# VectorE's slot reordered, and turned norms taken by ScalarE, in a four-layer attention and expert kernel

## The chip, the cores and the metric

One Trainium2 chip, one core. The metric is device time in microseconds of one execution. Each core has five engines with their own instruction streams: TensorE (PE), VectorE (DVE), ScalarE (ACT), GpSimd (POOL) and SyncE (SP, which here only issues DMAs). They meet at semaphores.

## The reference

The input is x of 32 sequences x 128 positions x 128 features, a condition vector per sequence and a context of 77 tokens per sequence. Four layers follow each other:

```python
# L0: self attention with rope and a mask, cross attention with the context, perceptron
x_norm = _ln(x, norm1_w) * (1 + sc_msa) + sh_msa
x = x + g_msa * self_out
xc = _ln(x, normc_w) * (1 + sc_x) + sh_x
x = x + g_x * cross
xm = _ln(x, norm2_w) * (1 + sc_mlp) + sh_mlp
x = x + g_mlp * (gelu(xm @ mlp_W1 + mlp_b1) @ mlp_W2 + mlp_b2)
# L1: evidence from the context, three routed experts, a gate
# L2: cross attention; queries and keys both from modulated norms
# L3: self attention, cross attention (of x without a norm), perceptron
```

Attention has 16 heads of 8 features, softmax over the keys. All is float32. Every modulated norm ends in a scale and a shift per feature and sequence.

## The kernel before

Four sequences make a quad; attention runs over 40 quads (5 attention layers x 8): l0 (128 keys, masked by the 128x128 mask, rope), l0c (77 keys, masked by a context mask), then, after the expert stage, l2 (77 keys), l3s (128 keys) and l3c (77 keys). The two phases are quads 0 to 15 and 16 to 39. Every engine has its own function `attention(phase, first, last)` that walks over slots t, one per sequence; `qi, cl = divmod(t, 4)` are the quad and the place in it (cl 0 to 3). Each engine's order within a slot is written out by hand, and semaphore waits tie the engines.

TensorE's slot t (lines 720 to 767): row scores of sequence t+5, half 1 (`rows`, L573: queries on partitions, only for the maxima); the exact scores of t transposed (`exact`, L604) and minus the maxima (`shift`, L616); row scores of t+6, half 0; `weigh` of t-1 (L631: probabilities times values). Then come `turn_max` at cl 3 (L581), and `quad_work`: at cl 0 the projection of the keys of quad qi+2 (L522, with rope also L525), at cl 1 the transpose of a norm (`turn_normed`, L490) or of x (L497), at cl 2 the values of qi+1 (L530) and the output projection of qi-2 (L537), at cl 3 the queries of qi+3 (L511, L514) and the transpose of a "family" norm (of the l2 context or of the two perceptrons). In the masked layer l0 the order is `quad_work` first and `weigh` and `turn_max` last. The two halves of row scores share two PSUM banks: `rows` waits until VectorE has taken the maximum of the half before it.

VectorE's slot t (lines 1227 to 1289): the maximum of t+5, half 1 (`row_max`, L1104); of t-2 the 32x32 block transpose of `weigh`'s result (`turn_blocks`, L1120); the transpose back of t-3 (`turn_back`, L1139); the reciprocal of the sums (`invert`, L1125); the maximum of t+6, half 0; at cl 3 `spread_max` (L1111, `nblk`); the product with the reciprocal (`normalise`, L1131, `attn`). Then `rotate` (rope, L1078 and L1082), `take_x` (L1068), `residual` at cl 2 (L1147, L1150), `take_q` at cl 3 (L1092, L1097), `scale_normed` (L1060) and `take_stats` (L978 and L983: four instructions each). In masked slots the first maximum stands behind `invert`, and `spread_max` behind the scaling.

A norm's way: `take_stats` on VectorE, Ln and Exp on ScalarE (`root`, L1454 and L1457), subtraction and product on GpSimd (`normalise_x`, L1679 and L1682), four transposes on TensorE into one PSUM bank (`turn_normed`), the scaling on VectorE from PSUM into `hat` (`scale_normed`), and the shift on GpSimd in the next slot from `hat` into the target (`shift_normed`, L1693). There are 56 of them: 24 in phase 0 and 32 in phase 1, 16 of those in phase 1 and 8 of those in phase 0 of the family kind. The PSUM bank is free again when `ln_scaled` has counted.

ScalarE's slot t: the exponentials of t (two instructions, L1508), taking keys (L1480, L1482) and values (L1498), `root`, `round_q` (L1471), taking queries (L1490). GpSimd's slot: `spread_q(t+1)` (L1655), adding the rotated half (L1672), `spread_k(t+7)` (L1665), `shift_normed`, `normalise_x`, adding bias rows or gated results (L1698, L1704).

The expert stage (`routed`, 10 iterations) lies between the phases; in its last iterations the first slots of phase 1 are interleaved by hand, on each engine at its own places. GpSimd cannot read PSUM here; all PSUM readers are VectorE and ScalarE.

Of the kernel before, what the change touches and what calls it, by code (L numbers as in the profile page):

```python
# [164 lines left out]
def build(nc, a, out_x):  # L165
    with ExitStack() as ctx:
# [62 lines left out]
        hat = sb("hat", [128, QUAD * S])  # L229
# [33 lines left out]
        ln_centred, ln_xhat, ln_turned, ln_scaled, ln_done = sem("ln_centred"), sem("ln_xhat"), sem("ln_turned"), sem("ln_scaled"), sem("ln_done")  # L263
# [183 lines left out]
        def tensor_program(e):  # L447
# [210 lines left out]
            def attention(phase, first=-16, last=None):  # L658
# [5 lines left out]
                def scores_read(t):  # L664

                    qi, cl = divmod(t, QUAD)
                    if cl == 0 and qi + 2 in quads and layer_of(qi + 2).rope:
                        w.wait_ge(rope_half, 4 * (qi + 2) + 4)
                    if t in norm_at and norm_at[t].family:
                        w.wait_ge(ln_scaled, norm_at[t].index + 1)  # L670
                    if cl == 2 and qi - 2 in quads and qi >= hi:
                        w.wait_ge(wo_read, qi - 1)
                    if cl == 2 and qi + 1 in quads:
                        w.wait_ge(v_done, qi + 2)
                    if cl == 3 and qi + 3 in quads and layer_of(qi + 3).rope:
                        w.wait_ge(rope_half, 4 * (qi + 3) + 2)

                def quads_read(t):

                    qi, cl = divmod(t, QUAD)  # L680
                    if cl == 0 and qi + 2 in quads:
                        if layer_of(qi + 2).rope:
                            w.wait_ge(rope_half, 4 * (qi + 2) + 3)
                        else:
                            w.wait_ge(k_done, qi + 2 - NB + 1)
                    if cl == 1 and qi + 3 in quads and layer_of(qi + 3).name == "l3c":
                        w.wait_ge(raw_done, (qi + 3) % NB + 1)
                    if t in norm_at and not norm_at[t].family:
                        w.wait_ge(ln_scaled, norm_at[t].index + 1)
# [169 lines left out]
            def routed():  # L859
# [8 lines left out]
                for i in range(NB + 2):  # L868
# [48 lines left out]
                    if last:  # L917
                        hidden_layer(c, 6)
                        if c == NB - 1:
                            w.wait_ge(ln_scaled, A_NORMS + 3)  # L920
                        gate_layer(c)
# [48 lines left out]
        def vector_program(e):  # L970
# [83 lines left out]

            def scale_normed(it):
                scale, _, ready, value = affine(it)
                w.wait_ge(ready, value)
                w.wait_ge(ln_turned, it.index + 1)
                w.wait_ge(ln_done, it.index)
                e.tensor_tensor(by_seq(hat[:, 0:it.cols]), by_seq(turned_bank(it)[:, 0:it.cols]),  # L1060
                                scale.unsqueeze(2).to_broadcast([128, QUAD, it.n]), ALU.mult).then_inc(ln_scaled, 1)
# [160 lines left out]
            def attention(phase, first=-16, last=None):  # L1222
# [3 lines left out]
                jobs, quads, norm_at = range(4 * lo, 4 * hi), range(lo, hi), NORM_AT[phase]  # L1226
                for t in range(4 * lo + first, end):
                    qi, cl = divmod(t, QUAD)
                    masked = t in jobs and layer_of(qi).mask == "qk"
                    if t + 5 in jobs and not masked:  # L1230
                        row_max(t + 5, 1)
                    if t - 2 in jobs:
                        turn_blocks(t - 2)
                    if t - 3 in jobs:
                        turn_back(t - 3)
                    if t - 2 in jobs:
                        invert(t - 2)
                    if t + 5 in jobs and masked:
                        row_max(t + 5, 1)
                    if t + 6 in jobs:  # L1240
                        row_max(t + 6, 0)
                    if cl == 3 and qi + 1 in quads and not masked:
                        spread_max(qi + 1)
                    if t - 2 in jobs:
                        normalise(t - 2)
                    if cl == 0 and qi + 2 in quads and layer_of(qi + 2).rope:
                        rotate(qi + 2, 1)
                    if cl == 1 and qi + 3 in quads and layer_of(qi + 3).name == "l3c":
                        take_x(qi + 3)
                    if cl == 2 and qi - 2 in quads:  # L1250
                        residual(qi - 2)
                    if cl == 3 and qi + 3 in quads:
                        if layer_of(qi + 3).rope:
                            rotate(qi + 3, 0)
                        elif not q_by_act(qi + 3):
                            take_q(qi + 3)
                    if t in norm_at:
                        scale_normed(norm_at[t])
                    if cl == 3 and qi + 1 in quads and masked:
                        spread_max(qi + 1)  # L1260
                    for it in STATS_AT.get((phase == 1, t), ()):
                        take_stats(it)
# [182 lines left out]
        def scalar_program(e):  # L1445
# [39 lines left out]

            def take_q(q):
# [25 lines left out]
            def attention(phase, first=-16, last=None):  # L1512
# [4 lines left out]
                for t in range(4 * lo + first, end):  # L1517
# [14 lines left out]
                    if cl == 2 and qi + 1 in quads:  # L1532
                        take_v(qi + 1)
                    for it in roots:
                        if not it.family:
                            root(it)
                    if cl == 1 and qi + 2 in quads:
                        round_q(qi + 2)
# [50 lines left out]
            for i in range(NB + 2):  # L1589
# [18 lines left out]
                if i + 1 < NB:  # L1608
                    routed_root(i + 1)
                if last:  # L1610
                    hidden_silu(c, 2)
                if now:
                    take_weights(i)
                if last:
# [3 lines left out]
                for k in (4, 5, 6):  # L1618
                    if last:
                        hidden_silu(c, k)  # L1620
                if last:
                    gate_sigmoid(c)
                if i == NB:
                    attention(1, -14, -7)
# [6 lines left out]
        def pool_program(e):  # L1631
# [53 lines left out]
            def shift_normed(it):  # L1685
                _, shift, ready, value = affine(it)
                w.wait_ge(ready, value)
                w.wait_ge(ln_scaled, it.index + 1)
                if it.kind in ("l2k", "l2", "l0", "l0c", "l3s"):
                    w.wait_ge(proj_v, it.q - 2)  # L1690
                    w.wait_ge(proj_q, it.q - 2)
                    w.wait_ge(proj_k, it.q - 2)
                e.tensor_tensor(by_seq(norm_target(it)), by_seq(hat[:, 0:it.cols]),  # L1693
                                shift.unsqueeze(2).to_broadcast([128, QUAD, it.n]), ALU.add).then_inc(ln_done, 1)

# [10 lines left out]
            def attention(phase, first=-16, last=None):  # L1706
# [4 lines left out]
                for t in range(4 * lo + first, end):  # L1711
# [9 lines left out]
                    if t - 1 in norm_at:  # L1721
                        shift_normed(norm_at[t - 1])
# [231 lines left out]
```

## Time and profile before

| | |
|---|---|
| median of 3 runs | 1201.91 us (1200.75 to 1204.64) |
| profiled execution | 1201.14 us, its span 1199.0 us |
| granted TensorE clock, mean | 0.954 |
| TensorE busy | 1068.0 us (89%) |
| VectorE busy | 821.1 us (68%) |
| ScalarE busy | 571.5 us (48%) |
| GpSimd busy | 598.0 us (50%) |
| chain that ended last | TensorE 66%, VectorE 20%, issue 7%, ScalarE 3%, GpSimd 3% |

Phase 0 takes about the first 400 us, the expert stage until about 675, phase 1 the rest. Busy shares are over the whole span. Matmul ends are modelled, and a busy TensorE is not TensorE at its peak; idle time of an engine costs only where others wait for it.

### The profile page before, as it was taken

The numbers are of one execution on the slowest core, as the hardware profiler recorded it, in microseconds if no ns is written. First come the engines' busy times: TensorE is split into PE (matmuls) and PEld (weight loads), VectorE is DVE, ScalarE is ACT, GpSimd is POOL, SyncE is SP. The second block draws the span as 40 slices with busy tenths as digits, with TensorE's granted clock in tenths as the row PEclk, the third lists the DMA queues.
The fourth block names the chain that finished last, engine by engine and source line by source line (L and its number), as shares of the span: only waits on it lengthen the run. The fifth ranks groups of instructions, "written<-read, shape, count | busy, mean of one in ns | idle before, by whom it ended". The sixth has DMA issues, their size and how long they took to land.

```text
span 1199.0 us, 28596 instructions
## 1 busy us (share of the span) xinstructions
PE 1068.0 (89%) x11711; PEld 674.1 (56%) x11711; DVE 821.1 (68%) x2035; ACT 571.5 (48%) x801; POOL 598.0 (50%) x602
## 2 busy tenths in 40 slices
PE   7899999999888997989999688899888999999898
PEld 4445545555554774656666445555555556655476
DVE  6677777778774433756677668788887887787521
ACT  1133334465556434443444236465555556665563
POOL 5565665566754331111114468576565645566421
PEclk8899999999999997998999769899999999998999
DMA  4300000000001102000000000000000000000001
GB/s 171 125 2 2 19 11 11 19 11 19 16 14 29 36 27 83 12 6 6 6 6 12 11 12 2 1 2 2 2 1 1 2 2 2 2 2 2 1 27 44
DMA packets 9280, 22.88 MB, mean 19 GB/s; under 512 B 1392, under 2 KB 1648, under 8 KB 8768
## 3 DMA queue, kind: packets, MB, share of 16 engines
q1 hardware_dynamic: 9152, 21.07, 5.3%
q8 instruction: 93, 1.52, 0.6%
q14 instruction: 35, 0.29, 0.1%
HBM read 18.90 MB, written 2.15 MB: 18 GB/s over the span
## 4 chain that ended last, share of the span: by engine, by line
PE 66%; DVE 20%; issue 7%; ACT 3%; POOL 3%; DMA 0%; DVEq 0%; SPq 0%; POOLq 0%; ACTq 0%
PE weighed L631 10%; DVE negmax L1104 9%; PE row_scores L573 6%; PE scores L777 5%; PE scores L604 5%; PE weighed L654 5%; PE scores L530 4%; PE quads L511 3%; PE quads L537 3%; PE quads L522 3%; PE row_scores L777 3%; DVE bn L978 2%; PE scores L616 2%; PE row_scores L788 2%; PE scores L644 2%
## 5 line engine op out<-in xcount | busy, mean ns | idle before, releaser
L1104 DVE TENSOR_REDUCE negmax<-row_scores 128x8 f32<-128x616 f32 (+1 forms) x312 | 298.6, 957 | 83.7 <-PE row_scores L573 52.4
L1508 ACT ACTIVATE p<-scores 128x1024 f32<-128x1024 f32 (+1 forms) x256 | 247.6, 1018 | 218.7 <-PE scores L616 218.7
L1665 POOL TENSOR_TENSOR kblk_r<-work,pack_const 128x308 fp32r<-128x308 f32 (+1 forms) x160 | 134.2, 839 | 240.7 <-PE row_scores L573 216.4
L604 PE MATMUL scores<-qblk,work 32*77 32x512 f32 (+1 forms) x1280 | 205.8, 626 | 13.9 <-ACT p L1508 6.8
L573 PE MATMUL row_scores<-kblk_r,qr 32*128 32x308 f32 (+1 forms) x624 | 141.9, 444 | 54.3 <-DVE negmax L1104 51.6
L631 PE MATMUL weighed<-p,v 77*32 77x128 f32 (+1 forms) x5120 | 176.1, 279 | 2.7 <-DVE nat L1120 2.5
L1655 POOL TENSOR_TENSOR qblk<-work,pack_const 128x512 f32<-128x512 f32 x160 | 168.7, 1054 | 14.6 <-PE scores L604 13.6
L573 PEld LDWEIGHTS row_scores<-kblk_r,qr 32*128 32x128 f32 x624 | 63.8, 189 | 176.0 <-issue 101.9
L631 PEld LDWEIGHTS weighed<-p,v 77*32 77x32 f32 (+1 forms) x5120 | 132.1, 111 | 45.7 <-DVE nat L1120 22.0
L616 PE MATMUL scores<-nblk,select 32*77 32x512 f32 (+1 forms) x640 | 154.9, 808 | 0.0
L1508 ACT ACTIVATE p<-scores,neg_kb 77x1024 f32<-77x1024 f32 x64 | 67.6, 1105 | 52.3 <-PE scores L616 52.3
L604 PEld LDWEIGHTS scores<-qblk,work 32*77 32x77 f32 (+1 forms) x1280 | 63.0, 161 | 22.5 <-ACT p L1508 9.6
L1120 DVE STREAM_TRANSPOSE nat<-weighed 128x256 f32<-128x256 f32 x160 | 70.2, 439 | 6.1 <-PE weighed L631 6.1
L1131 DVE TENSOR_TENSOR attn<-nat,rden 128x128 f32<-128x128 f32 x160 | 72.6, 454 | 0.5
L1679 POOL TENSOR_TENSOR xh<-x,mv 128x512 f32<-128x512 f32 x48 | 50.1, 1043 | 45.4 <-ACT rst L1457 45.4
L1748 POOL TENSOR_TENSOR xh<-x,r_mv 128x512 f32<-128x512 f32 x8 | 8.3, 1044 | 109.4 <-ACT r_rst L1465 109.4
L654 PEld LDWEIGHTS weighed<-layers_w,work 128*128 128x128 f32 x512 | 59.0, 192 | 5.3 <-issue 3.3
L654 PE MATMUL weighed<-layers_w,work 128*128 128x128 f32 x512 | 60.0, 275 | 1.6 <-DVE x L1168 0.8
L616 PEld LDWEIGHTS scores<-nblk,select 32*77 32x77 f32 (+1 forms) x640 | 47.3, 163 | 23.7 <-issue 13.5
L1682 POOL TENSOR_TENSOR xh<-xh,rst 128x512 f32<-128x512 f32 (+1 forms) x56 | 58.3, 1041 | 4.4
L511 PE MATMUL quads<-work,layers_w 128*128 128x512 f32 x80 | 49.2, 700 | 0.0
L1498 ACT COPY v<-scores 77x512 f32<-77x512 f32 (+1 forms) x40 | 23.4, 584 | 49.6 <-PE scores L530 49.6
(287 smaller groups left out, 1841.9 us busy)
## 6 DMA issues: line engine op xcount, KB each, us to landing
shared<-gates_hbm SPq DMA_DIRECT2D x24, 256.0 KB, 3.2
shared<-in_ctx_tok SPq DMA_DIRECT2D x16, 154.0 KB
pack_w_l<-in_w_l SPq DMA_DIRECT2D x1, 2058.5 KB, 10.0
x<-in_x_tok SPq DMA_DIRECT2D x8, 256.0 KB, 6.2
out_x<-x SPq DMA_DIRECT2D x8, 256.0 KB, 2.0
layers_w<-in_w_l SPq DMA_DIRECT2D x1, 1289.0 KB, 9.1
ctxT<-in_ctxT SPq DMA_DIRECT2D x1, 1232.0 KB, 8.8
layers_w<-in_w_l SPq DMA_DIRECT2D x1, 640.0 KB, 6.4
```

The source lines that it names most:

```text
L511: e.matmul(quad_bank[:, :], W[layer.wq], xn[q % 3], start=True, stop=True).then_inc(proj_q, 1)
L573: mm = e.matmul(row_banks(n, h)[:, i, 0:cols], qr[q % 3][at, s * S:(s + 1) * S], kblk_r[n % 2][at, 0:cols], start=layer.mask is None or ma ...
L604: mm = e.matmul(scores[0:nk, g, :], k_of[q % 3][at, s * nk:(s + 1) * nk], qblk[n % 2][at, :], start=layer.mask != "qk", stop=False, skip_g ...
L616: mm = e.matmul(scores[0:nk, g, :], select[at, s, 0:nk], nblk[q % 2][at, :], start=False, stop=True, skip_group_check=True, tile_position= ...
L631: mm = e.matmul(av_bank[TILE * j:TILE * j + TILE, i2 * S:(i2 + 1) * S], v[0:nk, at:at + TILE], p[n % 2][0:nk, g * NJ + j, :], start=i1 == ...
L654: mm = e.matmul(mlp_out_bank[:, s * D:(s + 1) * D], mlp_h[c % 2][k][:, s * S:(s + 1) * S], W[weight][:, k * D:(k + 1) * D], start=(k == 0) ...
L777: mm = e.matmul(bank, weight, src, start=(part == 0), stop=(part == 1))
L1104: e.tensor_reduce(negmax[q % 2][:, 2 * h:2 * h + 2, 0, s * NJ:(s + 1) * NJ], row_banks(n, h)[:, :, 0:NJ * nk].rearrange("p g (j k) -> p g ...
L1131: e.tensor_tensor(attn[n % 2][:, :].rearrange("p (k d) -> p k d", d=HD), nat[n % 2][:, :, :].rearrange("p i (k c) -> p (i k) c", c=16)[:, ...
L1508: e.activation(p[n % 2][0:nk, 8 * h:8 * h + 8, :], scores[0:nk, 2 * h:2 * h + 2, :].rearrange("p g (j q) -> p (g j) q", j=NJ), ACT.Exp, bi ...
L1655: e.tensor_tensor(qblk[n % 2][:, :].rearrange("p (j s) -> p j s", j=NJ), q_of[q % 3][:, s * S:(s + 1) * S].unsqueeze(1).to_broadcast([128, ...
L1665: e.tensor_tensor(kblk_r[n % 2][:, 0:NJ * nk].rearrange("p (j k) -> p j k", j=NJ), k_of[q % 3][:, s * nk:(s + 1) * nk].unsqueeze(1).to_bro ...
```

## The change

On VectorE the slot gets one order for masked and unmasked slots: both maxima first; then `rotate` for keys and for queries, `spread_max`; then the evacuation, of t-1 instead of t-2 (and the transpose back of t-2 instead of t-3), with reciprocal and `normalise` directly behind it; then `take_stats`; then `take_x`, `residual` and `take_q`. `scale_normed` is gone from VectorE and `shift_normed` from GpSimd. In their place ScalarE has `take_normed`: four activations per norm (one per sequence, 128 or 77 columns, scale and bias per partition) straight from PSUM into the target, behind the exponentials, `take_k`, `take_v` and `round_q` of the slot. TensorE waits for `ln_done` where it waited for `ln_scaled`. `round_q` moves ahead of the roots that are not of the family. In the expert stage ScalarE's slots -14 to -7 of phase 1 are spread between the activations of the last but one iteration.

```diff
@@ vector_program, attention @@
-                    masked = t in jobs and layer_of(qi).mask == "qk"
-                    if t + 5 in jobs and not masked:
-                        row_max(t + 5, 1)
-                    if t - 2 in jobs:
-                        turn_blocks(t - 2)
-                    if t - 3 in jobs:
-                        turn_back(t - 3)
-                    if t - 2 in jobs:
-                        invert(t - 2)
-                    if t + 5 in jobs and masked:
+                    if t + 5 in jobs:
                         row_max(t + 5, 1)
                     if t + 6 in jobs:
                         row_max(t + 6, 0)
-                    if cl == 3 and qi + 1 in quads and not masked:
-                        spread_max(qi + 1)
-                    if t - 2 in jobs:
-                        normalise(t - 2)
                     if cl == 0 and qi + 2 in quads and layer_of(qi + 2).rope:
                         rotate(qi + 2, 1)
+                    if cl == 3 and qi + 3 in quads and layer_of(qi + 3).rope:
+                        rotate(qi + 3, 0)
+                    if cl == 3 and qi + 1 in quads:
+                        spread_max(qi + 1)
+                    if t - 1 in jobs:
+                        turn_blocks(t - 1)
+                    if t - 2 in jobs:
+                        turn_back(t - 2)
+                    if t - 1 in jobs:
+                        invert(t - 1)
+                        normalise(t - 1)
+                    for it in STATS_AT.get((phase == 1, t), ()):
+                        take_stats(it)
                     if cl == 1 and qi + 3 in quads and layer_of(qi + 3).name == "l3c":
                         take_x(qi + 3)
                     if cl == 2 and qi - 2 in quads:
                         residual(qi - 2)
-                    if cl == 3 and qi + 3 in quads:
-                        if layer_of(qi + 3).rope:
-                            rotate(qi + 3, 0)
-                        elif not q_by_act(qi + 3):
-                            take_q(qi + 3)
-                    if t in norm_at:
-                        scale_normed(norm_at[t])
-                    if cl == 3 and qi + 1 in quads and masked:
-                        spread_max(qi + 1)
-                    for it in STATS_AT.get((phase == 1, t), ()):
-                        take_stats(it)
+                    if cl == 3 and qi + 3 in quads and not layer_of(qi + 3).rope and not q_by_act(qi + 3):
+                        take_q(qi + 3)
@@ scalar_program @@
+            def take_normed(it):
+                scale, shift, ready, value = affine(it)
+                w.wait_ge(ready, value)
+                w.wait_ge(ln_turned, it.index + 1)
+                if not it.kind in ("l0m", "l3f"):
+                    w.wait_ge(proj_v, it.q - 2)
+                    w.wait_ge(proj_q, it.q - 2)
+                    w.wait_ge(proj_k, it.q - 2)
+                for s in range(QUAD):
+                    at = slice(s * it.n, (s + 1) * it.n)
+                    done = e.activation(norm_target(it)[:, at], turned_bank(it)[:, at], ACT.Identity, bias=shift[:, s:s + 1],
+                                        scale=scale[:, s:s + 1])
+                done.then_inc(ln_done, 1)
@@ scalar_program, attention @@
+                    if cl == 1 and qi + 2 in quads:
+                        round_q(qi + 2)
+                    if t in norm_at:
+                        take_normed(norm_at[t])
                     for it in roots:
                         if not it.family:
                             root(it)
-                    if cl == 1 and qi + 2 in quads:
-                        round_q(qi + 2)
@@ scalar_program, expert stage @@
+                if i == NB:
+                    attention(1, -14, -12)
                 if last:
                     hidden_silu(c, 2)
...
                 if i == NB:
-                    attention(1, -14, -7)
+                    attention(1, -8, -7)
@@ tensor_program, four places @@
-                        w.wait_ge(ln_scaled, norm_at[t].index + 1)
+                        w.wait_ge(ln_done, norm_at[t].index + 1)
@@ pool_program @@
-                    if t - 1 in norm_at:
-                        shift_normed(norm_at[t - 1])
```

## Rows read from the trace of the kernel before

**Rows 1.** Waits of TensorE, whole span: waiting, releaser: total us, times, longest.
```profile
PE row_scores L573 <- DVE negmax L1104: 51.6, 75, 2.8
...
PE scores L604 <- DVE hat L1060: 6.4, 7, 1.1
```

**Rows 2.** Timeline in l3s, cl 2 to cl 0: start, us, engine, line, tiles, idle before.
```profile
880.94 0.50 PE L573 MATMUL row_scores<-kblk_r,qr 32*128 32x512 f32 x2 [0.66 <-DVE negmax L1104]
...
884.36 0.50 PE L573 MATMUL row_scores<-kblk_r,qr 32*128 32x512 f32 x2
...
884.47 0.69 DVE L1150 TENSOR_TENSOR x<-quads,x 128x512 f32<-128x512 f32 x1 [1.57 <-PE quads L537]
...
886.27 1.19 DVE L1104 TENSOR_REDUCE negmax<-row_scores 128x8 f32<-128x1024 f32 x1
...
887.61 0.50 PE L573 MATMUL row_scores<-kblk_r,qr 32*128 32x512 f32 x2 [1.65 <-DVE negmax L1104]
...
889.42 0.69 DVE L1111 TENSOR_TENSOR nblk<-weighed,pack_const 128x512 fp32r<-128x512 f32 x1
...
890.17 0.49 PE L573 MATMUL row_scores<-kblk_r,qr 32*128 32x512 f32 x2
...
890.71 1.23 DVE L1104 TENSOR_REDUCE negmax<-row_scores 128x8 f32<-128x1024 f32 x1 [0.40 <-PE row_scores L573]
...
890.75 1.04 POOL L1665 TENSOR_TENSOR kblk_r<-work,pack_const 128x512 fp32r<-128x512 f32 x1 [3.77 <-PE row_scores L573]
...
891.85 0.44 DVE L1120 STREAM_TRANSPOSE nat<-weighed 128x256 f32<-128x256 f32 x1
...
892.08 0.50 PE L573 MATMUL row_scores<-kblk_r,qr 32*128 32x512 f32 x2 [0.32 <-DVE negmax L1104]
...
894.58 0.50 PE L573 MATMUL row_scores<-kblk_r,qr 32*128 32x512 f32 x2
```

**Rows 3.** Timeline at the end of phase 0, VectorE without row maxima.
```profile
367.81 0.45 DVE L1120 STREAM_TRANSPOSE nat<-weighed 128x256 f32<-128x256 f32 x1 [1.25 <-PE weighed L631]
...
368.62 0.29 DVE L1131 TENSOR_TENSOR attn<-nat,rden 128x128 f32<-128x128 f32 x1
...
368.83 0.86 DVE L978 BATCH_NORM_STATS2 bn<-x 128x6 f32<-128x128 f32 x4
```

**Rows 4.** Timeline late in l3c: a product beside a GpSimd operation.
```profile
1105.27 1.27 POOL L1698 TENSOR_TENSOR x<-x,rows_bc 128x512 f32<-128x512 f32 x1
...
1105.58 1.10 DVE L1131 TENSOR_TENSOR attn<-nat,rden 128x128 f32<-128x128 f32 x1
```

**Rows 5.** Timeline in the masked layer l0, from cl 2 to the next quad.
```profile
142.49 1.08 PE L631 MATMUL weighed<-p,v 128*32 128x128 f32 x32
...
144.05 0.50 PE L573 MATMUL row_scores<-kblk_r,qr 32*128 32x512 f32 x2
...
145.06 1.16 DVE L1104 TENSOR_REDUCE negmax<-row_scores 128x8 f32<-128x1024 f32 x1
...
146.37 0.50 PE L573 MATMUL row_scores<-kblk_r,qr 32*128 32x512 f32 x2 [0.73 <-DVE negmax L1104]
...
150.44 0.69 DVE L1111 TENSOR_TENSOR nblk<-weighed,pack_const 128x512 fp32r<-128x512 f32 x1 [0.51 <-PE weighed L581]
...
151.47 1.04 POOL L1665 TENSOR_TENSOR kblk_r<-work,pack_const 128x512 fp32r<-128x512 f32 x1 [0.18 <-PE row_scores L573]
```

**Rows 6.** Groups by shape, whole span: busy us, mean ns, idle before.
```profile
L1104 DVE TENSOR_REDUCE negmax<-row_scores 128x8 f32<-128x616 f32 x188 | 148.3, 789 | 36.2 <-PE row_scores L573 34.9 <-PE scores L573 1.1
...
L1490 ACT ACTIVATE work<-quads,layers_w 128x512 f32<-128x512 f32 x21 | 14.4, 688 | 34.8 <-PE quads L511 34.8
...
L1454 ACT ACTIVATE logv<-mv,eps_col 128x4 f32<-128x4 f32 x48 | 14.1, 294 | 30.2 <-DVE mv L983 30.1
```

**Rows 7.** Timeline, end of phase 1 and expert stage: two waits.
```profile
1133.06 1.08 PE L631 MATMUL weighed<-p,v 77*32 77x128 f32 x32 [1.23 <-DVE nat L1120]
...
659.98 0.46 PE L490 MATMUL scores<-pack_const,xh 77*128 77x77 f32 x4 [2.28 <-POOL xh L1682]
```

More of the change, by code:

```diff
@@ L228, in build @@
         xh = [sb(f"xh{f}", [128, QUAD, D]) for f in range(2)]
-        hat = sb("hat", [128, QUAD * S])
         gated = [sb(f"gated{i}", [128, QUAD * D]) for i in range(2)]
@@ L262, in build @@
         ln_bn, ln_stats, ln_log, ln_rstd = ([sem(f"{s}{f}") for f in range(2)] for s in ("ln_bn", "ln_stats", "ln_log", "ln_rstd"))
-        ln_centred, ln_xhat, ln_turned, ln_scaled, ln_done = sem("ln_centred"), sem("ln_xhat"), sem("ln_turned"), sem("ln_scaled"), sem("ln_done")
+        ln_centred, ln_xhat, ln_turned, ln_done = sem("ln_centred"), sem("ln_xhat"), sem("ln_turned"), sem("ln_done")
         raw_turned, raw_done = sem("raw_turned"), sem("raw_done")
@@ L688, in quads_read @@
                     if t in norm_at and not norm_at[t].family:
-                        w.wait_ge(ln_scaled, norm_at[t].index + 1)
+                        w.wait_ge(ln_done, norm_at[t].index + 1)
                     if cl == 2 and qi - 2 in quads and qi < hi:
@@ L919, in routed @@
                         if c == NB - 1:
-                            w.wait_ge(ln_scaled, A_NORMS + 3)
+                            w.wait_ge(ln_done, A_NORMS + 3)
                         gate_layer(c)
@@ L1053, in setup_gates @@
                 e.tensor_copy(live_bc[:, :], av_bank[:, 3 * D + B:3 * D + 2 * B]).then_inc(dve_setup, 1)
[L1055 to L1061, printed above, removed]
             def take_x(q):
@@ L1225, in attention @@
                 end = 4 * hi + TAIL if last is None else 4 * lo + last
-                jobs, quads, norm_at = range(4 * lo, 4 * hi), range(lo, hi), NORM_AT[phase]
+                jobs, quads = range(4 * lo, 4 * hi), range(lo, hi)
                 for t in range(4 * lo + first, end):
                     qi, cl = divmod(t, QUAD)
-                    masked = t in jobs and layer_of(qi).mask == "qk"
-                    if t + 5 in jobs and not masked:
-                        row_max(t + 5, 1)
-                    if t - 2 in jobs:
-                        turn_blocks(t - 2)
-                    if t - 3 in jobs:
-                        turn_back(t - 3)
-                    if t - 2 in jobs:
-                        invert(t - 2)
-                    if t + 5 in jobs and masked:
+                    if t + 5 in jobs:
                         row_max(t + 5, 1)
@@ L1613, in scalar_program @@
                     take_weights(i)
+                if i == NB:
+                    attention(1, -12, -10)
                 if last:
@@ L1617, in scalar_program @@
                     take_evidence(i)
-                for k in (4, 5, 6):
-                    if last:
-                        hidden_silu(c, k)
                 if last:
+                    hidden_silu(c, 4)
+                    hidden_silu(c, 5)
+                if i == NB:
+                    attention(1, -10, -8)
+                if last:
+                    hidden_silu(c, 6)
                     gate_sigmoid(c)
                 if i == NB:
-                    attention(1, -14, -7)
+                    attention(1, -8, -7)
                 if i + 1 < NB:
@@ L1683, in normalise_x @@
                                 ALU.mult).then_inc(ln_xhat, 1)
[L1685 to L1694, printed above, removed]
             def add_rows(c, row, done):
```

## The prediction

> **What bounds the kernel now.** I read the waits of TensorE first, then the groups by shape, then the timeline of single slots. TensorE is busy 89% of the span, and its largest wait by far is for a row maximum of VectorE: 51.6 us in 75 waits, then 6.4 us for the scaled norm [rows 1]. So the kernel is TensorE in its fixed order, plus what VectorE is late. A slot has two couplings: the row scores of half 1 open it, the row scores of half 0 of the next sequence stand behind `exact` and `shift`, and the second may not start before the maximum of the first is taken.
>
> I measure in a 128-key slot of the third-phase self attention [rows 2]. Row scores begin at P = 890.17; the maximum can begin at P + 0.54 (890.71); the second row scores begin 1.37 after it (892.08). With VectorE on time the second pair starts at Q = P + 1.91. Each microsecond that VectorE comes after P + 0.54 is a microsecond of TensorE: at P = 884.36 the maximum starts at 886.27, 1.37 late, and the second pair at 887.61 instead of 886.27, with 1.65 idle [rows 2]. So the question is: when is VectorE free, relative to P + 0.54 of the next slot?
>
> **The change part by part.** *Order.* Before, the evacuation (transpose, transpose back, reciprocal) of sequence t-2 stands in the gap between the two maxima, where VectorE would wait for TensorE anyway: a maximum advances it 1.14 (890.71 to 891.85), and the next one can start only at Q + 0.54, that is 1.91 after the last began, a gap of 0.8. After, that gap is empty and the evacuation of t-1 follows the second maximum. Its length is read where nothing disturbs it: transpose at 367.81, `attn` at 368.62 (0.81 later, 0.29 long), the next instruction at 368.83: 1.02 in all [rows 3]. VectorE is then free at Q + 0.54 + 1.14 + 1.02 = Q + 2.70. Four slots of a quad, with P' the next slot's start:
> - cl 0: P' = Q + 2.50 (894.58), limit Q + 3.04: on time, before and after.
> - cl 1: P' = Q + 2.02 by the same view, limit Q + 2.56: 0.14 late; before, with the 0.60 of the scaling, 0.34.
> - cl 2: P' = Q + 3.42 (880.94 to 884.36), limit Q + 3.96. Before: residual from 0.11 after the end slot begins (884.47), then statistics (0.90 + 0.30 by cadence), maximum 1.37 late. After: statistics go ahead, into the wait for the output projection, then the residual 0.60: free at Q + 2.70 + 1.20 + 0.60 = Q + 4.50, 0.54 late. This is the gain of the change: 0.83.
> - cl 3: before on time. After, `nblk` (at Q + 1.81, 889.42) comes first, 0.60, and the 1.02 behind it: free at Q + 3.43 against 3.10, 0.33 late.
> By this alone a quad gains 0.7 us.
>
> *Contention.* But `attn` now begins at Q + 1.81 + 0.60 + 0.81 = Q + 3.22, which is P' + 0.66 (P' = 890.17), and GpSimd's key spread starts at P' + 0.58 (890.75) and runs 1.04. A normal `attn` takes 0.29; the one at 1105.58 that met a GpSimd operation (1105.27 for 1.27) took 1.10 and ended 0.14 after it [rows 4]. So `attn` ends at P' + 1.76, and VectorE is free at P' + 1.68, 1.14 late in place of 0.33. The margin is 0.08 us, so both values stay as bounds. The Trainium skill (SBUF — State Buffer, Summary: rules for kernel authors) states it outright: a VectorE operation with two SBUF inputs and a GpSimd operation that reads SBUF block each other fully, the second to issue waiting. The trace agrees (1.10 against 0.29) [rows 4]; if instead `attn` issued first, the rule would give the 0.33.
>
> *The same by layer*, lateness per quad before and after:
> - l0 (masked, 8 quads). Here `weigh` is TensorE's last work of a slot, so the evacuation waits for it, and all that is queued behind comes later still. cl 2: `weigh` ends at 142.49 + 1.08 = 143.57; evacuation from 143.61 to 144.63, statistics to 145.83, residual to 146.43, limit 144.05 + 0.54 = 144.59: 1.84 late, where before the maximum started at 145.06, 0.47 late (idle 0.73) [rows 5]. cl 3: `nblk` at 150.44 as before, then the transpose at 151.04 and `attn` at 151.85, inside the key spread of 151.47: free at 152.58, 1.16 late against 0.31. Sum 3.1 against 0.86: 2.25 x 6 = 13.5. The first two quads have no residual: 2.0 x 2 = 4.0. Three quads take Q at the very end of cl 3: 0.6 x 3 = 1.8. In all +19.3.
> - l0c (77 keys; a maximum advances VectorE 0.70 by its 789 ns [rows 6]). The limit rule is the same with zero slack. Four quads win at cl 2 (1.41 to 0.5) and lose at cl 3 (`nblk`, evacuation, taking Q); where statistics fall on cl 1 they now add to the whole evacuation (0.2 to 1.2). About -1.4.
> - l2: the four late quads 1.71 to 1.45, two 2.9 to 1.8, the first two (no residual) +0.7 each: -1.8.
> - l3s: 1.71 to 1.80 in four quads, +0.9 in one, and three quads that have `take_x` at cl 1 and no statistics, 0.37 to 2.04: +6.3.
> - l3c: `take_x` now stands behind the evacuation (0.26 to 0.68) and cl 3 costs 0.82: three quads +1.25, two +0.43, two with statistics alone +1.0: +6.6.
>
> *The four activations.* No 128-column activation from PSUM is in the trace. From below it is 0.29 (the 4-column one), from above 0.69 (512 columns) [rows 6]; linear between them, 0.39, and 0.28 from start to start as far as the two overlap: 4 cost 1.2, bounds 0.8 and 2.8. The Trainium skill (ScalarE: Activation LUTs, Rules for kernel authors) gives 0.3 us plus 0.83 ns per element, 0.41 each, so 1.6 for four, an estimate; the sum would be some 0.4 us per place that waits higher. The scalings are in the working above (0.60 of VectorE's queue, as `nblk`); GpSimd's shifts had nothing waiting. ScalarE has room between two exponentials except in 77-key slots, where rounding Q plus four activations end some 0.5 after the next exponential could start and `project_v` waits 0.2: 8 places, 1.6. Family norms hold a scores bank that `exact` waits for: before 1.1 from the turn to the scaled copy, now 1.35; about 6 places, 1.5. Sum +3.1, bounds 0 and +20.
>
> *Ends and the routed stage.* At the end of each phase a `weigh` waits 1.23 for a transpose queued behind a scaling [rows 7]; the transpose now comes a slot sooner: -2.4, and -1.0 for a GpSimd shift before the last perceptron. In the routed stage the turn of a norm waits 2.28 for GpSimd [rows 7], of which one shift (1.0) goes, and two scalings leave VectorE's last chain: -2.0. The start waits 0.5 longer for the first norm.
>
> Sum: 19.3 - 1.4 - 1.8 + 6.3 + 6.6 + 3.1 - 3.4 - 2.0 + 0.5 = +27. The profiled execution took 1201.14 (span 1199.0 and 2.1 around it); the median is 1201.91. Forecast 1228, own range 1217 to 1240.
>
> **The rivals.**
> 1. *No collision on the port.* The margin of 0.08 falls the other way, or GpSimd, relieved of 56 shifts, keeps clear. Then cl 3 costs 0.33 (0.4 with 77 keys): 6.6 less in l3s, 4.2 in l0, 4.0 in the other three: +12, 1214. For it: the small margin in l3s. Against: 0.38 of overlap in l0.
> 2. *Maxima first serves TensorE* (faster). The place is cl 2: if the statistics really vanish into the wait for the output projection and the evacuation fits behind the second maximum everywhere, waits above the 0.32 that each 128-key slot has by structure go. The waits for maxima are 51.6, of which some 60 x 0.32 = 19 stay; taking half of the other 33, and 5 of the 6.4, it is -21: 1180. It decides once VectorE's free time stays under Q + 3.0; my count has it over in cl 2 and cl 3.
> 3. *ScalarE becomes a bound*: activations of 0.69 each, 2.8 per norm, would meet the exponentials at 56 places with 0.2 to 1.5: +12 on the forecast, 1240. Against: 0.29 for a small one.
> 4. *No change*: gains and losses cancel, 1202. For it: l0c and l2 do cancel.
>
> **How the numbers follow.** Forecast 0.46, rival 1 0.25, rival 3 0.09, rival 2 0.13, rival 4 0.07. The range leaves out the faster case and the top of rival 3: 1203 to 1242. Within 0.3% (3.6 us) is what a measurement can't tell from no change. Faster 0.13, same 0.06, slower 0.81.
>
> **What would show it.** In the masked layer the maximum of half 1 after cl 2 starts 1.8 after its row scores end, not 0.5, and TensorE's wait there grows from 0.73 to about 2.1; the quad is 2.2 longer. In l3s the quads with statistics keep their length, with the wait at cl 3 down from 1.65 to 0.85 and that at cl 0 up from 0.32 to 1.4, behind an `attn` of about 1.1. TensorE's waits for maxima rise from 51.6 to above 75 in all. VectorE's busy time falls by some 38, GpSimd's by 58, and ScalarE's rises by 224 x 0.39 = 87. I am wrong if the masked quad does not grow, since 19 of the 27 lie there.

## The result, and the profile after

The changed kernel takes 1318.45 us (1314.34 to 1323.98, 4 runs) against 1203.15 of the kernel before (4 runs): ratio 1.0963, 95% interval 1.0917 to 1.101. It is 115 us slower, where 27 were forecast. The profiled execution has a span of 1317.6 us; the granted clock falls from 0.954 to 0.912.

The page of the changed kernel: busy time by engine, and the chain that ended last.

```profile
PE 1122.1 (85%) x11711; PEld 702.3 (53%) x11711; DVE 815.7 (62%) x1979; ACT 648.6 (49%) x1025; POOL 544.6 (41%) x546
...
PE 61%; DVE 24%; issue 7%; ACT 5%; POOL 3%; DMA 0%; DVEq 0%; ACTq 0%; POOLq 0%
```

TensorE runs the same 11711 matmuls, and is busy 54.1 us longer with them. That is the first half of the loss. The second is in the waits (engine, line, tile, what it waited for, total us, times, longest). First TensorE's, then VectorE's:

```profile
PE row_scores L572 <- DVE negmax L1095: 99.3, 84, 3.2
PE row_scores L567 <- DVE negmax L1095: 26.6, 18, 2.5
...
PE scores L603 <- ACT normT L1479: 6.5, 6, 1.8
```

```profile
DVE attnT L1130 <- PE quads L536: 53.3, 30, 3.2
```

The first two rows, together 125.9, answer to the 51.6 of [rows 1] and to this row of the kernel before, for masked row scores, whose first matmul is another line:

```profile
PE row_scores L568 <- DVE negmax L1104: 9.4, 10, 1.3
```

Before it was 61.0 in all. The waits for maxima rise by 64.9, and 64.9 + 54.1 = 119.0 is, within 0.4, the 118.6 by which the span grew. VectorE's row is new: before, its transpose back never waited for the output projection; there it was the residual that did.

Stretches by layer, each from one `nblk` to another, for l0, l0c, l2, l3s, l3c. The l0 line ends with the `nblk` of l0's last quad and the l0c line with that of l0c's last, so that the last masked quad is counted in the l0c line. The l2 and l3s lines run from a layer's first `nblk` to that of the next layer, the l3c line to its last quad. Columns: stretch, length, busy us of the engines, granted clock, DMA share, GB/s. Before:

```profile
52.34:219.62 167.28, 153.55 (x2391) 84.91 (x2390) 126.42 (x261) 65.07 (x85) 98.78 (x94) 0.99 0.05 13
219.62:363.81 144.19, 129.91 (x1915) 80.38 (x1909) 111.15 (x292) 80.56 (x104) 91.97 (x98) 0.98 0.05 16
...
697.34:848.15 150.81, 134.98 (x1707) 80.20 (x1706) 119.81 (x308) 84.39 (x119) 103.10 (x109) 0.93 0.01 3
848.15:1001.24 153.09, 136.10 (x1737) 85.36 (x1736) 123.11 (x248) 83.01 (x104) 88.55 (x87) 0.98 0.01 2
1001.24:1116.95 115.71, 110.03 (x1515) 68.51 (x1514) 87.06 (x219) 69.43 (x89) 71.66 (x75) 0.97 0.01 2
```

After:

```profile
57.58:249.91 192.33, 162.18 (x2379) 88.29 (x2379) 127.01 (x252) 74.94 (x113) 92.20 (x87) 0.93 0.03 9
249.91:420.82 170.91, 143.89 (x1915) 87.85 (x1910) 111.42 (x284) 92.83 (x140) 82.41 (x88) 0.88 0.05 13
...
752.53:923.91 171.38, 145.80 (x1707) 87.10 (x1706) 115.99 (x296) 101.86 (x173) 91.73 (x96) 0.86 0.01 2
923.91:1098.53 174.62, 144.49 (x1737) 89.55 (x1737) 128.50 (x243) 89.99 (x124) 83.59 (x82) 0.92 0.01 2
1098.53:1232.92 134.39, 115.19 (x1515) 71.99 (x1514) 90.91 (x216) 73.51 (x101) 68.37 (x72) 0.94 0.01 2
```

Every line is 19 to 27 us longer, not that of the masked layer alone, and in each TensorE's busy time grows with the length. With all eight quads (52.34 to 238.74 before, 57.58 to 273.54 after) the masked layer goes from 186.4 to 216.0, and l0c without the masked quad from 125.1 to 147.3.

The slot at fault, in l3s (timeline of the changed kernel, cl 2 to cl 0, the counterpart of [rows 2]):

```profile
985.00 1.06 PE L536 MATMUL quads<-layers_w,attnT 128*128 128x128 f32 x8
...
985.99 0.50 PE L572 MATMUL row_scores<-kblk_r,qr 32*128 32x512 f32 x2
...
986.16 0.31 DVE L1130 STREAM_TRANSPOSE attnT<-attn 128x128 f32<-128x128 f32 x1 [1.48 <-PE quads L536]
...
986.57 1.04 POOL L1671 TENSOR_TENSOR kblk_r<-work,pack_const 128x512 fp32r<-128x512 f32 x1 [3.39 <-PE row_scores L572]
986.65 1.11 DVE L1122 TENSOR_TENSOR attn<-nat,rden 128x128 f32<-128x128 f32 x1
...
987.68 0.86 DVE L977 BATCH_NORM_STATS2 bn<-x 128x6 f32<-128x128 f32 x4
...
988.87 0.66 DVE L1141 TENSOR_TENSOR x<-quads,x 128x512 f32<-128x512 f32 x1
...
989.45 1.21 DVE L1095 TENSOR_REDUCE negmax<-row_scores 128x8 f32<-128x1024 f32 x1
...
990.81 0.50 PE L572 MATMUL row_scores<-kblk_r,qr 32*128 32x512 f32 x2 [3.23 <-DVE negmax L1095]
...
992.80 1.92 PE L510 MATMUL quads<-work,layers_w 128*128 128x512 f32 x2
```

`attnT` has two buffers. At cl 2 the order of before turned back the last sequence of quad qi-1, into the buffer whose projection (that of quad qi-3) had long been done. The new order is one sequence ahead: at cl 2 it turns back the first sequence of quad qi, into the buffer that the output projection of quad qi-2 still reads, and TensorE issues that projection at the end of this very slot. So VectorE stands idle from 984.68 to 986.16, and only then do the transpose back, reciprocal, `attn` (1.11, beside the key spread), statistics and residual run, all in a row. The maximum, which could begin at 985.99 + 0.54 = 986.53, begins 2.92 late.

Behind this wait the two matmuls of the query projection take 1.92. In the kernel before they took 1.02 behind a wait of 1.65:

```profile
889.22 1.02 PE L511 MATMUL quads<-work,layers_w 128*128 128x512 f32 x2
```

The stretches of two microseconds there, in the changed kernel (last column but two is the granted clock):

```profile
987.00:989.00 2.00, 0.57 (x8) 0.00 (x0) 1.97 (x10) 1.57 (x2) 1.65 (x2) 1.00 0.02 4
989.00:991.00 2.00, 0.19 (x2) 0.21 (x2) 1.66 (x2) 0.76 (x3) 0.00 (x0) 1.00 0.00 0
991.00:993.00 2.00, 2.00 (x36) 1.38 (x35) 1.22 (x1) 0.00 (x0) 0.00 (x0) 0.72 0.04 8
993.00:995.00 2.00, 2.00 (x7) 0.50 (x9) 1.67 (x5) 0.25 (x1) 0.00 (x0) 0.50 0.00 0
995.00:997.00 2.00, 1.68 (x16) 0.93 (x12) 1.23 (x1) 1.05 (x2) 1.48 (x2) 0.92 0.00 0
```

TensorE is idle from 987.58 to 990.81. The row scores at 990.81 still take 0.50. From about 991.9 to about 995.2, although TensorE is fully busy, the clock stands at its lower level (0.50 of 2.4 GHz, that is 1.2 GHz). The wait costs its 3.23 us, and the matmuls that follow it take longer on top.

### The profile page after: what moved, and what is told of

It reads as the page before. It is cut to its first block, busy times and chain, and to the rows that moved or that the text cites. A ratio compares the mean times of both kernels' runs of the same rounds, so it can differ in the third digit from the quotient of the medians.

```text
span 1317.6 us, 28587 instructions
## 1 busy us (share of the span) xinstructions
PE 1122.1 (85%) x11711; PEld 702.3 (53%) x11711; DVE 815.7 (62%) x1979; ACT 648.6 (49%) x1025; POOL 544.6 (41%) x546
## 3 DMA queue, kind: packets, MB, share of 16 engines
q8 instruction: 93, 1.52, 0.5%
## 4 chain that ended last, share of the span: by engine, by line
PE 61%; DVE 24%; issue 7%; ACT 5%; POOL 3%; DMA 0%; DVEq 0%; ACTq 0%; POOLq 0%
PE weighed L630 12%; DVE negmax L1095 8%; PE row_scores L572 5%; PE scores L776 5%; PE scores L603 4%; PE weighed L653 4%; PE scores L529 4%; PE quads L510 3%; PE quads L536 3%; DVE bn L977 3%; PE quads L521 2%; PE row_scores L776 2%; DVE attn L1122 2%; DVE nat L1111 2%; ACT p L1505 2%
## 5 line engine op out<-in xcount | busy, mean ns | idle before, releaser
L572 PE MATMUL row_scores<-kblk_r,qr 32*128 32x308 f32 (+1 forms) x624 | 149.7, 469 | 102.5 <-DVE negmax L1095 99.3
L603 PE MATMUL scores<-qblk,work 32*77 32x512 f32 (+1 forms) x1280 | 220.4, 663 | 13.8 <-ACT p L1505 6.7
L630 PE MATMUL weighed<-p,v 77*32 77x128 f32 (+1 forms) x5120 | 191.5, 295 | 3.5 <-ACT normT L1479 3.5
L572 PEld LDWEIGHTS row_scores<-kblk_r,qr 32*128 32x128 f32 x624 | 67.6, 202 | 229.3 <-issue 171.0
L630 PEld LDWEIGHTS weighed<-p,v 77*32 77x32 f32 (+1 forms) x5120 | 143.0, 117 | 55.3 <-issue 51.2
L615 PE MATMUL scores<-nblk,select 32*77 32x512 f32 (+1 forms) x640 | 161.4, 833 | 0.0
L1505 ACT ACTIVATE p<-scores,neg_kb 77x1024 f32<-77x1024 f32 x64 | 67.5, 1105 | 54.6 <-PE scores L615 54.6
L603 PEld LDWEIGHTS scores<-qblk,work 32*77 32x77 f32 (+1 forms) x1280 | 69.5, 173 | 22.6 <-ACT p L1505 9.6
L1130 DVE STREAM_TRANSPOSE attnT<-attn 128x128 f32<-128x128 f32 x160 | 44.5, 278 | 53.4 <-PE quads L536 53.3
L615 PEld LDWEIGHTS scores<-nblk,select 32*77 32x77 f32 (+1 forms) x640 | 50.9, 171 | 25.8 <-issue 15.1
L510 PE MATMUL quads<-work,layers_w 128*128 128x512 f32 x80 | 61.5, 862 | 0.0
L1688 POOL TENSOR_TENSOR xh<-xh,rst 128x512 f32<-128x512 f32 (+1 forms) x56 | 58.2, 1039 | 4.4
```

The costliest lines, as they stand in the source:

```text
L510: e.matmul(quad_bank[:, :], W[layer.wq], xn[q % 3], start=True, stop=True).then_inc(proj_q, 1)
L572: mm = e.matmul(row_banks(n, h)[:, i, 0:cols], qr[q % 3][at, s * S:(s + 1) * S], kblk_r[n % 2][at, 0:cols], start=layer.mask is None or ma ...
L603: mm = e.matmul(scores[0:nk, g, :], k_of[q % 3][at, s * nk:(s + 1) * nk], qblk[n % 2][at, :], start=layer.mask != "qk", stop=False, skip_g ...
L615: mm = e.matmul(scores[0:nk, g, :], select[at, s, 0:nk], nblk[q % 2][at, :], start=False, stop=True, skip_group_check=True, tile_position= ...
L630: mm = e.matmul(av_bank[TILE * j:TILE * j + TILE, i2 * S:(i2 + 1) * S], v[0:nk, at:at + TILE], p[n % 2][0:nk, g * NJ + j, :], start=i1 == ...
L1505: e.activation(p[n % 2][0:nk, 8 * h:8 * h + 8, :], scores[0:nk, 2 * h:2 * h + 2, :].rearrange("p g (j q) -> p (g j) q", j=NJ), ACT.Exp, bi ...
```

## The experiments

Each ran beside the kernel before on its own chip (1200.16 us for the first four, 1200.84 for the next four, 1201.04 for the last three).

**1. Three buffers for attnT** (the changed kernel otherwise).

```diff
-        attnT = [sb(f"attnT{i}", [128, QUAD * S]) for i in range(2)]
+        attnT = [sb(f"attnT{i}", [128, QUAD * S]) for i in range(3)]
-                w.wait_ge(wo_done, q - 1)          # and attnT[q % 2] -> attnT[q % 3]
+                w.wait_ge(wo_done, q - 2)
```

> The changed kernel with a third attnT buffer, so that the transpose back of a quad's first sequence no longer waits in cl 2 for the output projection two quads back. Theory A (this wait, overlooked in the prediction, moves statistics and residual of the four unmasked layers behind the output projection): the 53.3 us that VectorE waits for L536 go to under 5, TensorE's wait at cl 3 of l3s goes from 3.2 to about 0.9, the four unmasked layers lose some 2 us per quad x 30 = 60 and the half-clock stretches behind these waits another 10 to 25, the masked layer keeps its 192 us: 1225 to 1255. Theory B (the loss is the order as such, evacuation behind both maxima, and the port): the wait only changes its name, over 1295.

Measured 1254.8 us (ratio 1.0457, 1.0422 to 1.0493): 64 us of the loss gone with one tile (61 if each is compared with the kernel before on its own chip, 54.6 above it in place of 115.3). VectorE's transpose back no longer waits for the output projection; the residual does, for 15.6 us in all. The l3s slots of this run (timeline), cl 2 to cl 0:

```profile
963.21 0.27 DVE L1130 STREAM_TRANSPOSE attnT<-attn 128x128 f32<-128x128 f32 x1
...
965.06 0.66 DVE L1141 TENSOR_TENSOR x<-quads,x 128x512 f32<-128x512 f32 x1
...
965.63 1.21 DVE L1095 TENSOR_REDUCE negmax<-row_scores 128x8 f32<-128x1024 f32 x1
...
966.99 0.50 PE L572 MATMUL row_scores<-kblk_r,qr 32*128 32x512 f32 x2 [0.81 <-DVE negmax L1095]
...
970.21 1.12 DVE L1122 TENSOR_TENSOR attn<-nat,rden 128x128 f32<-128x128 f32 x1
...
972.61 0.50 PE L572 MATMUL row_scores<-kblk_r,qr 32*128 32x512 f32 x2 [1.47 <-DVE negmax L1095]
```

This is the slot that the prediction described: 0.85 forecast for the first wait, 0.81 found; 1.4 behind an `attn` of 1.1 for the second, 1.47 and 1.12 found. The lengths of l0c, l2, l3s and l3c come down by 19.0, 20.3, 17.4 and 6.3; l0, which has no such wait, keeps its 192.3.

**2. The norms alone** (before's order on VectorE without the scaling, the activations on ScalarE, with the rest of what the change does on ScalarE, GpSimd and TensorE) and **3. the order alone** (the new order on VectorE, scaling and shift left with VectorE and GpSimd).

> VectorE's order as before the change, the norms by the four activations on ScalarE and nothing on GpSimd, as after it. If ScalarE's activations are harmless, as predicted: 1190 to 1205, 34 us less on VectorE's queue giving a few us back at cl 1. If they are a main cause of the loss: over 1240.

> VectorE's order as after the change, norms scaled on VectorE (at the end of the slot) and shifted on GpSimd as before. If the order is the whole loss: 1310 to 1345 (the scaling adds 0.6 behind the evacuation at cl 1). If order and activations share the loss: under 1290.

Measured 1193.05 (ratio 0.9942, 0.992 to 0.9964) and 1340.72 (1.1157, 1.111 to 1.1204). The order is the whole loss, and what moves to ScalarE is a small gain on either side: 7 us by itself, 22 within the new order (25 by the differences to the kernel before). VectorE's busy time falls by 38.4 with the norms alone, exactly the forecast 38; that the changed kernel shows only 5.4 less is therefore due to the order. Of the missing 33 us, 12 are a longer `attn` (475 ns mean against 401) and 3 other instructions. The other 18 are no work: neighbouring instructions overlap less. The durations of all of VectorE's instructions add to 858.4 for 782.7 of busy time in experiment 2 and to 873.0 for 815.7 in the changed kernel.

**4. More work for TensorE, none taken away**: in the changed kernel a helper issues `matmul(bank, ident, ones)` four times (eight matmul records in the trace, results overwritten) in each of 28 slots, ahead of `exact` at cl 3 of the unmasked layers, just before TensorE's wait for the maximum, so that the wait becomes shorter.

```diff
+                if s == 3 and layer.mask != "qk" and q + 2 < (2 * NB if q < 2 * NB else NQ):
+                    keep_busy(4, scores[:, 0, 0:128])
                 for g in range(NG):
```

> The changed kernel with four more 128x128 matmuls per quad on TensorE, ahead of exact at cl 3 of the unmasked layers, whose results are overwritten. They lie within the 3.2 us that TensorE waits there for a row maximum. If the idle stretch brings TensorE's half clock behind it (theory C, granted clock 0.88 in l0c and 0.86 in l2 against 0.98 and 0.92 before): the clock of the unmasked layers rises by 0.03 or more, the masked layer stays at 0.93, and the time falls by 8 to 30 us although work is added: 1290 to 1310. If the clock has another cause: unchanged clock, 1318 to 1325.

Measured 1300.75 (ratio 1.0855, 1.0792 to 1.0918): 18 us less with 224 matmuls more (15 less by the differences to the kernel before on either chip; the two 95% intervals of the ratio only just touch). Granted clock and length: l0c from 0.88 to 0.97 and 170.9 to 161.2, l2 from 0.86 to 0.97 and 171.4 to 159.4, l3s from 0.92 to 0.97 and 174.6 to 171.2, l3c from 0.94 to 0.96, less than the 0.03 expected, while l0, which got none, has 0.91 and 194.8. In l3s the wait behind the filler is still 1.9 in five quads, and the query projection behind it takes 1.92, 1.82, 1.79 and 1.26 in four of them, 1.02 in the fifth. TensorE's busy time is within 0.6 that of the changed kernel (1122.7), with the added work in it.

**5. Key spread kept behind attn** (on top of three buffers).

```diff
                 w.wait_ge(rows_done, 2 * n - 2)
+                w.wait_ge(attn_done, n - 8)
                 e.tensor_tensor(kblk_r[n % 2]...
```

> On top of the three attnT buffers (1254.8 us): GpSimd's key spread additionally waits until VectorE's attn of the same stretch is written, so that the two no longer read SBUF side by side. Theory A (collision on the port): with three buffers the slot of the third-phase self attention at cl 0 has the wait of 1.47 us behind an attn of 1.12 us beside a key spread; kept apart, attn takes 0.29 and the maximum can start up to 0.75 sooner, once per quad in the 128-key layers, some 32 quads x 0.4 to 0.75 = 13 to 24 us with what the clock gives back: 1231 to 1242, the waits for maxima (95 us) down to about 80. Theory B (the collision only shifts idle time): the spread itself comes late and TensorE waits for kblk_r in its place: 1250 or more, with waits for kblk_r above 10 us.

Measured 1233.32 (1.0274, 1.0236 to 1.0313), 21 us less than experiment 1. The same slots (timeline):

```profile
950.62 0.29 DVE L1122 TENSOR_TENSOR attn<-nat,rden 128x128 f32<-128x128 f32 x1
950.83 1.22 DVE L1095 TENSOR_REDUCE negmax<-row_scores 128x8 f32<-128x1024 f32 x1
951.06 1.04 POOL L1672 TENSOR_TENSOR kblk_r<-work,pack_const 128x512 fp32r<-128x512 f32 x1 [3.43 <-DVE attn L1122]
...
952.19 0.49 PE L572 MATMUL row_scores<-kblk_r,qr 32*128 32x512 f32 x2 [0.64 <-POOL kblk_r L1672]
```

`attn` is back to 0.29 and the wait of 1.47 is 0.64. Both theories hold in part: the waits for maxima fall from 95.1 to 63.0 (about 80 expected), but those for `kblk_r` rise from 1.9 to 21.4 in 43. What the Trainium skill says of this port (SBUF — State Buffer, Summary: rules for kernel authors), that the second to issue waits out the first, agrees with 1.12 (experiment 1, where the spread had started at 970.14 and `attn` at 970.21) against 0.29 for the same instruction.

**6. The masked slots' evacuation as before** (on top of three buffers: for t in l0, `turn_blocks(t - 2)`, `turn_back(t - 3)` and `invert(t - 2)` ahead of the maxima again, `normalise(t - 2)` behind them; at the first slot of l0c both orders meet).

> On top of the three attnT buffers (1254.8 us): in the 32 masked slots of the first layer alone the evacuation is that of sequence t-2 again and stands ahead of the maxima, as in the kernel before; the rest of the order stays new. Theory A (the order costs the masked layer 19 us, because weigh is TensorE's last work of a slot and the evacuation of t-1 behind it holds the next maximum): the first layer falls from 192.3 to 167 to 175 us, and the whole to 1230 to 1238. Theory B (the loss of the masked layer comes from nblk, the rotation halves or the norms, not from the evacuation): the layer stays above 185 and the whole above 1247.

Measured 1228.34 (1.0223, 1.0185 to 1.0261), 26 us less than experiment 1 and 2 below the expected range. All of it is in the masked layer, whose line is:

```profile
61.22:224.44 163.22, 149.79 (x2379) 83.59 (x2379) 121.20 (x251) 74.94 (x113) 91.84 (x87) 1.00 0.03 10
```

That is 29.0 less than in experiment 1; with all eight quads it is 33.3 less (215.8 to 182.5).

**7 and 8. The kernel before with the statistics ahead of the residual**, and the same with the norms on ScalarE.

```diff
+                    for it in STATS_AT.get((phase == 1, t), ()):
+                        take_stats(it)
                     if cl == 2 and qi - 2 in quads:
                         residual(qi - 2)
...
-                    for it in STATS_AT.get((phase == 1, t), ()):
-                        take_stats(it)
```

> The kernel before with one edit: the statistics of the norms stand ahead of the residual in the slot instead of last. Theory A (what the change rightly saw: at cl 2 VectorE waits for the output projection with nothing to do, then runs residual and statistics in a row, so that the maximum is 1.37 us late): the statistics, 1.20 us, fit into that wait, the maximum is at most 0.2 late, and some 25 quads gain 0.8 to 1.2 us: 20 to 30 us less, 1172 to 1182. Theory B (the residual then comes later and wo_read or the next norm's chain takes the place of the wait): no change, 1196 to 1206.

> The kernel before with the statistics ahead of the residual and the turned norms scaled and shifted by four activations on ScalarE, VectorE's order otherwise as before. Theory A: both gains add, that of the norms alone being 7 us (0.6 us less of VectorE's queue at each norm) and that of the statistics alone 20 to 30: 1163 to 1175. Theory B: with the statistics out of the way the scaling no longer stands in the critical slot, so that the norms give nothing more: the same as with the statistics alone, within 3 us.

Measured 1169.84 (0.9739, 0.9709 to 0.9769) and 1167.17 (0.9715, 0.9687 to 0.9743). One move of two lines gives 31 us, 2 more than the range expected. In experiment 8 (timeline, l3s, cl 2 to cl 3):

```profile
884.57 0.87 DVE L977 BATCH_NORM_STATS2 bn<-x 128x6 f32<-128x128 f32 x4
...
886.22 0.69 DVE L1141 TENSOR_TENSOR x<-quads,x 128x512 f32<-128x512 f32 x1 [0.37 <-PE quads L536]
...
886.83 1.22 DVE L1095 TENSOR_REDUCE negmax<-row_scores 128x8 f32<-128x1024 f32 x1
...
888.19 0.50 PE L572 MATMUL row_scores<-kblk_r,qr 32*128 32x512 f32 x2 [0.49 <-DVE negmax L1095]
```

The statistics lie inside the wait for the projection, and the 1.65 of [rows 2] is 0.49. This is the gain that the prediction credited to the change at cl 2; before's evacuation order lets it happen. The norms on ScalarE add 2.7 us, within the 3 of theory B and with overlapping intervals; the same kernel measured 1164.63 as experiment 10. Once the slot at cl 2 is free, moving the scaling gains at most a few us. These two are the fastest versions measured.

**9. All three repairs at once** (three buffers, key spread behind `attn`, masked slots as before).

> The changed kernel with all three repairs at once: three attnT buffers, the key spread held until attn is written, the masked slots with the old evacuation. Theory A (three separate causes, with the prices that the single runs gave: 64 us, 21 us, 26 us): they add, 1318 - 64 - 21 - 26 = 1207, between 1202 and 1214; what then stays over the 1193 of the old order with the norms on ScalarE is the evacuation at cl 3 and in 77-key slots. Theory B (they share the same waits, so that the repairs overlap): above 1216.

Measured 1210.63 (1.0073, 1.0051 to 1.0096): they add. The three causes are separate and account for 108 of the 115 us (106 by the differences to the kernel before). What stays over the 1193.05 of experiment 2, the old order with the norms on ScalarE, was not taken apart by a run. By the traces it lies in the start (+7.5) and in the 77-key layers (l0c +6.9, l2 +3.5, l3c +7.4), while l3s and the masked layer are 3.3 and 2.5 shorter.

**10 and 11. What a late maximum costs.** In experiment 11, on top of the kernel of experiment 8:

```diff
+                    if cl == 3 and t + 6 in jobs and not masked:
+                        for k in range(7):
+                            e.tensor_reduce(pad[:, 2 * k:2 * k + 2], cos_live[:, :, :], AX_X, ALU.max)
                     if t + 5 in jobs and not masked:
                         row_max(t + 5, 1)
```

Experiment 10 is the yardstick, the kernel of experiment 8 once more.

> The kernel with the statistics ahead of the residual and the norms on ScalarE, unchanged: the yardstick for the next run, in the same call. Theory A and B alike: 1163 to 1171.

> The kernel with the statistics first and the norms on ScalarE, and in the unmasked slots of cl 3 seven reductions of a 256-element table into a scratch tile ahead of the maximum of half 1: VectorE is late by some 2.3 us at this one slot of each of 32 quads (0.3 each by cadence, from 0.79 us for 616 elements), as in the changed kernel behind the transpose back. Nothing else changes. Theory A (a wait of 2 to 3 us costs more than its length, since TensorE's matmuls after it run at half clock): the waits give 32 x 2.3 = 74 us and TensorE's busy time grows by another 20 to 40, 1262 to 1282. Theory B (a wait costs its length): 1235 to 1245, TensorE's busy time within 5 us of 1056.5.

Measured 1164.63 and 1274.56 (1.0605, 1.0569 to 1.0641). Timeline of experiment 11:

```profile
958.71 2.37 DVE L1224 TENSOR_REDUCE pad<-cos_live 128x2 f32<-128x256 f32 x7
...
962.36 0.79 PE L573 MATMUL row_scores<-kblk_r,qr 32*128 32x512 f32 x2 [2.77 <-DVE negmax L1096]
...
965.21 1.91 PE L511 MATMUL quads<-work,layers_w 128*128 128x512 f32 x2
```

TensorE's waits for maxima, experiment 10 first, then experiment 11:

```profile
PE row_scores L572 <- DVE negmax L1095: 30.0, 69, 2.2
...
PE row_scores L573 <- DVE negmax L1096: 78.1, 70, 2.8
PE row_scores L568 <- DVE negmax L1096: 15.2, 8, 2.4
```

The 32 delays of 2.37 (two of them ahead of the masked layer) are 76 us of VectorE; the kernel is 110 us slower, and its profiled execution, the slowest of the four, 117. TensorE waits 62.5 us more for maxima (30.8, with 0.8 for masked row scores, to 93.3) and is busy 58.2 us longer with the same matmuls (1056.8 to 1115.0), more than the 20 to 40 of theory A. The mean granted clock goes from 0.966 to 0.918. So about half of what a wait of 2 to 3 us costs here is not the wait but the lower clock behind it.

## Why the prediction was wrong

The direction was right, the size was 27 against 115.

- **The step that failed: cl 2 of the unmasked layers.** "After: statistics go ahead, into the wait for the output projection, then the residual 0.60: free at Q + 2.70 + 1.20 + 0.60 = Q + 4.50, 0.54 late." In the trace the maximum there is 2.92 late. I had checked each moved instruction against the maxima and the port, but not the transpose back against its own waits. Moving it one sequence ahead moved it across a quad boundary of a two-buffered tile, so that at cl 2 the evacuation waits for the same projection as the residual. The statistics stand between the two and cannot fill the wait. Price with what follows from it: 64 us (experiment 1). With that wait away the slot is the one forecast, to 0.07 us.
- **A cost with no term: the clock.** The rule "Each microsecond that VectorE comes after P + 0.54 is a microsecond of TensorE" is too low. With three buffers the waits for maxima are 34.1 above before (61.0 to 95.1), near the 29.0 of my five layer terms, but TensorE's busy time is up another 23.1 and the kernel 54.6 longer. It could have been read from the kernel before: its l2 stands at 0.93, and in l3s the two matmuls of the query projection, 1.02 in most quads, take 1.76 at 868.65 and 1.52 at 910.10.
- **Masked layer, +19.3.** Right as to mechanism: the wait behind cl 2 is 2.14 (at 161.08; forecast 2.1), that of cl 0 1.46 (at 170.27) behind an `attn` of 0.81. Over its eight quads the waits for maxima rise by 20.5 (13.6 to 34.1), near the 19.3, and with the lower clock (0.99 to 0.93) the length by 29.6: 3.7 per quad where 2.2 were forecast. Experiment 6 takes back 33.3.
- **l3s +6.3, l3c +6.6.** With three buffers the waits rise by 5.3 and 6.7. Right as to waits.
- **l0c -1.4, l2 -1.8.** Even with three buffers l0c, without the masked quad, is +2.9 in waits (7.5 to 10.4) and l2 +0.6: small as forecast, but wrong in sign.
- **The port.** Right in the masked layer and in experiment 1. In the changed kernel itself it struck at cl 2, since the late transpose back pushed `attn` onto the key spread (986.57 and 986.65), and not at cl 0 (994.46, 0.29).
- **Four activations, +3.1.** 0.46 each, four in a row 1.5, near the 1.6 worked out from the Trainium skill (ScalarE: Activation LUTs, Rules for kernel authors) and above my 0.39 and 1.2. As a whole the norms are a gain of 7 (experiment 2): I had counted the relief of VectorE only inside the new order. ScalarE did not become a bound (rival 3). ScalarE's busy time rises by 77 (forecast 87), GpSimd's falls by 53 (58).
- **Start and ends.** The start, up to the first `nblk`, is 5.2 longer (0.5 forecast). In experiment 6, with the same order there as the changed kernel, it is 61.2 against 57.6, so that I leave its cause open. The last 82.0 became 84.7, where -3.4 for both ends was forecast; between the phases -1.8 (-2.0 forecast).

## What to carry to other kernels

When work is moved by one item within a software pipeline, list the semaphore that each moved instruction waits for, with its index at every position of the loop, and look for the index that crosses a buffer's boundary; one more buffer may be the whole repair. A wait already present is filled by moving independent work ahead of the waiting instruction, not by moving the waiting chain. And a wait of TensorE of 2 to 3 us, as here, is priced with the matmuls behind it, not by its length alone.

## What was not expected of the hardware

l3s with waits of up to 1.5 us had a granted clock of 0.99 (experiment 1). With one of 2.1 to 3.2 us per quad it had 0.91 to 0.92 (experiment 11, the changed kernel), and in most quads matmuls behind the wait ran at the lower level: up to 1.92 for the two that take 1.02 at the higher one, 0.79 for row scores of 0.50. Between the two it varies from quad to quad: behind a wait of 1.65 or 1.66 the kernel before has 1.76 and 1.52 in two quads and 1.02 in others. And work added to TensorE in that stretch made the kernel 18 us faster (experiment 4).
